# Relational graph convolution on one core: the aggregation buffer with relations outermost, ScalarE writing it with a step, TensorE reading runs of 72

## The reference, cut to what matters

```python
N, F_in = x.shape                    # 6250 nodes, 128 features, float32
R = W_rel.shape[0]                   # 65 relations; 200000 edges, sorted by dst
seg  = dst * R + edge_type
sums = segment_sum(x[src], seg, N * R).reshape(N, R, F_in)
cnt  = segment_sum(ones, seg, N * R).reshape(N, R, 1)
agg  = sums / maximum(cnt, 1.0)      # a mean for each (node, relation)
h = einsum('nri,rio->no', agg, W_rel) + x @ W_root + bias + x @ W_res + b_res
h = relu(batchnorm_over_nodes(h) * gamma + beta)
out = layernorm_over_features(x + h)
```

## Time and profile before

| | value |
|---|---|
| median of three runs | 2689.86 us |
| the profiled execution | 2688.44 us |
| its span (first to last instruction) | 2686.7 us |
| PE busy | 2594.1 us (97%) |
| DVE busy | 1681.9 us (63%) |
| POOL busy | 1471.8 us (55%) |
| ACT busy | 1311.1 us (49%) |
| mean granted TensorE clock | 0.993 of 2.4 GHz |

### The profile page before, as it was taken

How to read it: one execution, slowest core, us unless ns; L and a number is a source line. 1 busy time by engine, 2 the same in 40 slices (tenths; PEclk the granted TensorE clock), 3 DMA queues, 4 the chain that set the end, 5 groups by cost and what they waited for, 6 DMA issues and landing times.

```text
span 2686.7 us, 42326 instructions
## 1 busy us (share of the span) xinstructions
PE 2594.1 (97%) x12868; PEld 2271.2 (85%) x12868; DVE 1681.9 (63%) x5648; ACT 1311.1 (49%) x2427; POOL 1471.8 (55%) x1581
## 2 busy tenths in 40 slices
PE   2899999999999999999999999999999999999995
PEld 1688888888888888888888888888888888888884
DVE  4866666666666666666666665666666666666624
ACT  1545545545554454554545544545454454454523
POOL 2555555555555555555555555555555655555510
PEclk9999999999999999999999999999999999999998
DMA  8645454554445545444444554545545454554421
GB/s 293 175 122 138 117 131 124 131 131 121 130 121 133 132 117 136 119 129 127 127 130 116 138 132 117 136 116 131 138 117 131 121 134 125 123 131 114 116 72 49
DMA packets 262850, 345.30 MB, mean 129 GB/s; under 512 B 29051, under 2 KB 245311, under 8 KB 249439
## 3 DMA queue, kind: packets, MB, share of 16 engines
q0 software_dynamic: 225072, 204.97, 33.8%
q1 hardware_dynamic: 37551, 137.59, 15.3%
HBM read 328.84 MB, written 13.60 MB: 127 GB/s over the span
## 4 chain that ended last, share of the span: by engine, by line
PE 96%; DMA 1%; DVE 1%; ACT 1%; issue 1%; SPq 0%; POOL 0%; ACTq 0%; DVEq 0%; POOLq 0%
PE tb L571 65%; PE ps L546 21%; PE ps L552 8%; DMA xtab<-agg 1%; PE tb L530 1%; ACT agg L729 0%; PE tb L531 0%; DVE bst L1016 0%; PE ps L631 0%; DMA xg<-xtab,srcT 0%; DMA agg<-in_x_dram 0%; PE ps L632 0%; DVE agg L755 0%; PE tb L520 0%; PE prep L509 0%
## 5 line engine op out<-in xcount | busy, mean ns | idle before, releaser
L475 POOL DMA_INDIRECT xg<-xtab,srcT x1563 | 1467.7, 939 | 1096.4 <-PE ps L552 500.5
L571 PE MATMUL tb<-agg,wsb 128*128 128x144 f32 x6370 | 1972.2, 448 | 1.4 <-issue 1.4
L858 DVE TENSOR_SCALAR onehot<-iota,segT,v 128x456 fp32r<-128x456 f32 x1173 | 874.7, 746 | 856.1 <-PE ps L552 695.9
L662 ACT ACTIVATE agg<-ps 128x390 f32 (+1 forms) x1563 | 775.5, 496 | 1246.7 <-PE ps L552 970.8
L571 PEld LDWEIGHTS tb<-agg,wsb 128*128 128x128 f32 x6370 | 1167.8, 201 | 151.2 <-issue 1.5
L546 PE MATMUL ps<-onehot,xg 128*128 128x390 f32 (+1 forms) x3126 | 1155.0, 453 | 37.9 <-DMA xg<-xtab,srcT 35.1
L546 PEld LDWEIGHTS ps<-onehot,xg 128*128 128x128 f32 x3126 | 639.3, 207 | 191.8 <-DMA xg<-xtab,srcT 35.8
L832 DVE TENSOR_SCALAR_CACHE_REDUCE junk<-keyb,keyT 128x256 bf16<-128x256 f32 x1563 | 713.2, 471 | 2.7 <-DMA keyb<-keyd 2.7
L552 PEld LDWEIGHTS ps<-onehot,xg 128*128 128x128 f32 x2930 | 539.9, 189 | 3.8
L552 PE MATMUL ps<-onehot,xg 128*128 128x66 f32 x2930 | 448.0, 234 | 0.0
L651 ACT ACTIVATE onehot<-dist,v,negv 128x456 fp32r<-128x456 f32 x390 | 299.4, 768 | 36.9 <-ACT dist L646 0.7
(11 more groups left out here) (107 smaller groups left out, 353.4 us busy)
## 6 DMA issues: line engine op xcount, KB each, us to landing
keyb<-keyd SPq DMA_DIRECT2D x98, 1088.0 KB
xg<-xtab,srcT POOLq DMA_INDIRECT x1563
xtab<-agg SPq DMA_DIRECT2D x4, 1536.0 KB
hinit<-H SPq DMA_DIRECT2D x1, 3125.0 KB
agg<-in_x_dram SPq DMA_DIRECT2D x4, 768.0 KB, 9.0
out_dram<-agg SPq DMA_DIRECT2D x6, 448.0 KB, 3.0
srcr<-in_src_dram SPq DMA_DIRECT2D x12, 64.0 KB
dstr<-in_dst_dram SPq DMA_DIRECT2D x12, 64.0 KB
```

The costliest lines, as they stand in the source:

```text
L475: pool.indirect_dma_start(out=xg[c % RING][:], out_offset=None, in_=xtab.bitcast(F32R), in_offset=bass.IndirectOffsetOnAxis(ap=srcT[t % 2] ...
L571: ins = nc.tensor.matmul(o, wsb[:, r * F:(r + 1) * F], pair_rhs(p, r), start=(r == 0), stop=(r == R - 1))
L662: nc.scalar.activation(agg_group(g)[:, bass.ds(off, w)], ps[c % 4][:, 0:w], ACT.Copy).then_inc(evac, 1)
L858: nc.vector.tensor_scalar(onehot[o][:].rearrange("p (a b) -> p a b", a=3), iota3[:, :, 0:IW], segT[t % 2][:, k:k + 1], v[:, g % 2, j:j + 1 ...
```

## The change: relations outermost, the two groups' nodes side by side

In a half of `agg`, the column of relation `r`, group `g` (0 or 1) and node `n` is now `r * 156 + g * 78 + n`. The size is the same.

- `pair_rhs` reads, for one relation, 72 adjacent words of group 0, leaves out 6, and reads 72 adjacent words of group 1.
- `evacuate` reads PSUM as before, in order, and writes for each of 6 (or 7) nodes 65 words that are 156 words (624 bytes) apart. The number of elements is the same.
- The offset is now in nodes, so one small DVE instruction that multiplied it by 65 falls away (13 times in all), with the semaphore step before it. Nothing else is added, removed or moved: PE, ACT, POOL and SP issue the same instructions in the same order.

```diff
     OW = (SLOTS + 1) * R + 1
-    GREG = (WIN + SLOTS) * R
-    PREG = 2 * GREG
+    GN = WIN + SLOTS
+    PREG = 2 * GN * R
...
         def agg_group(g):
 
-            base = (g // 2 % 2) * PREG + (g % 2) * GREG
-            return agg[:, base:base + GREG]
+            base, n = (g // 2 % 2) * PREG, (g % 2) * GN
+            return agg[:, base:base + PREG].rearrange("f (r n) -> f n r", r=R)[:, n:n + GN, :]
...
             def turn_offsets(t):
                 pe.wait_ge(offc_rdy, t + 1)
-                nc.tensor.matmul(prep[0:1, 0:P], tc(T_OFF65), ident[:], start=True, stop=True)
+                nc.tensor.matmul(prep[0:1, 0:P], tc(T_OFF2), ident[:], start=True, stop=True)
...
             def pair_rhs(p, r):
                 a = (p % 2) * PREG
-                return agg[:, a:a + PREG].rearrange("f (g n r) -> f g n r", g=2, r=R)[:, :, 0:WIN, r]
+                return agg[:, a:a + PREG].rearrange("f (r g n) -> f r g n", r=R, g=2)[:, r, :, 0:WIN]
...
             def evacuate(c, off):
                 p, g = c // (2 * GC), c // GC
-                w = OW - 1 if last_of_group(c) else W6
+                n = SLOTS + 1 if last_of_group(c) else SLOTS
...
-                nc.scalar.activation(agg_group(g)[:, bass.ds(off, w)], ps[c % 4][:, 0:w], ACT.Copy).then_inc(evac, 1)
+                nc.scalar.activation(agg_group(g)[:, bass.ds(off, n), :],
+                                     ps[c % 4][:, 0:n * R].rearrange("f (n r) -> f n r", r=R), ACT.Copy).then_inc(evac, 1)
...
-                    offs = registers(offrow[t % 2][0:1, k:k + 4], ENG.Activation, (WIN - 1) * R)
+                    offs = registers(offrow[t % 2][0:1, k:k + 4], ENG.Activation, WIN - 1)
...
-                at = step(nc.vector.tensor_scalar(tc(T_OFF2), tc(T_OFF), 0.0, float(WIN - 1), ALU.max, ALU.min))
-                dve.wait_ge(dstep, at)
-                nc.vector.tensor_scalar(tc(T_OFF65), tc(T_OFF2), float(R), None, ALU.mult)
+                nc.vector.tensor_scalar(tc(T_OFF2), tc(T_OFF), 0.0, float(WIN - 1), ALU.max, ALU.min)
```

More of the change, by code:

```diff
@@ L163, in gnn @@
         (B_BIAS, B_RES, GAM, BET, BSUM, BAD, MV, STD, SCL, SHF) = (0, 1, 2, 3, 4, 5, 6, 8, 9, 10)
-        (T_B, T_NEXT, T_B65, T_LAST, T_BG, T_OFF, T_LASTG, T_OFF2, T_OFF65, T_RISE) = range(10)
+        (T_B, T_NEXT, T_B65, T_LAST, T_BG, T_OFF, T_LASTG, T_OFF2, T_RISE) = range(9)
         XST = (XT + 1) * 2 * F
```

## The result

The changed kernel takes 2514.64 us (median of 4 runs, 2509.71 to 2516.89), the kernel before 2689.49 us beside it: a ratio of 0.9347, 95% interval 0.9330 to 0.9363. That is 6.5% faster. The forecast was 2282 us with a range of 2080 to 2430, so the direction was right and the size was not: 233 us of the expected gain of 408 are missing. The profiled run had a span of 2513.6 us.

The account below looks back on a forecast made before the run. PE's pace bounded the kernel; after the change ACT would, at 1.36 us per chunk. Start 118, loop 2081, 6 to the last products, 18 for them, 55.8 to the end: 2279, with 1.7 and 1.4 added 2282 us, range 2080 to 2430.

Parts of the forecast that it names:

- The W_r products: PE's L571 products: reading runs of 72 adjacent words cuts each from 0.2615 to 0.127 us, PE's chunk to 1.07 us.
- ACT's stepped write: ACT's evacuation into SBUF: writing with a step takes 901 ns, 0.408 us more, making ACT's chunk 1.36 us.
- split into 199 ns and 1.80 ns per element: ACT's evacuation: 199 ns fixed plus 1.80 ns for each of 390 stepped elements, 901 ns together.
- SBUF and not the engine sets the price: Stepped access: DVE's writing (1.94 ns) and PE's reading (1.82) cost nearly the same, so 1.80 ns was taken for ACT.
- ACT as the bound: The loop: ACT sets the pace at 1.36 us per chunk (1.26 to 1.60), time 2282 us, chance 66%.
- ACT without idle time in the loop: Sign of being right: ACT's evacuations follow each other by their length plus 0.17 us.
- I am wrong if ACT's cycle grows by something other than the write: Stated sign of failure: ACT's four-chunk cycle lengthening by anything but its evacuations' stepped write.
- the 0.67 us of spare time per chunk: ACT's cover before the change: PE's 1.62 us per chunk less ACT's 0.95.
- Rival 1: POOL's gathers, 1.244 us apart, set the loop's pace if the stepped evacuation stays under 787 ns: 2089 us, chance 18%.
- Rival 3: PE's clock falls to half where PE idles behind ACT: 2770 us if half the time, 2400 one in eight; chance 8%.
- Rivals 2 and 4: ACT's evacuation over 1.17 us makes the kernel slower, 2740 us, 4%; runs of 72 stream no faster, 2690 us, 4%.
- 1.71 ns per column: The skill page's DVE price, tried for ACT's evacuation: 866 ns, 1.32 us per chunk, some 2230 us in all.

Follow-up runs that it names:

- write_only: Changed kernel with the old read, so only ScalarE's stepped write against the kernel before: 2694.22 us, ratio 1.0015.
- pool_on_evac: Changed kernel, but GpSimd waits before every fourth gather on evac, not agg_ps: 2211.59 us, ratio 0.8235 to the kernel before.
- dve_all: Changed kernel, but VectorE makes all one-hots and ScalarE only evacuates: 2088.83 us, ratio 0.7776 to the kernel before.
- filler: Changed kernel plus one float32 product per chunk into an unused PSUM bank, to keep TensorE busier: 2524.84 us, ratio 0.9392 to the kernel before.
- own_semaphore: Changed kernel, but GpSimd waits on its own semaphore, raised by TensorE at each chunk's first product: 2519.55 us, ratio 0.9354 to the kernel before.
- wait_on_memset: Changed kernel, but GpSimd's wait on agg_ps stands at a small memset ahead of every fourth gather: 2623.44 us, ratio 0.9752 to the kernel before.
- wait_each: Changed kernel, but GpSimd waits on agg_ps before every gather instead of once for four: 2475.14 us, ratio 0.9201 to the kernel before.
- read_only: Kernel before with only TensorE's new read of 72-word runs, ScalarE writing adjacent words as before: 2478.14 us, ratio 0.9211.
- read_dve_all: Kernel before with only TensorE's new read, and all one-hots made by VectorE: 2514.63 us, ratio 0.9341.
- no_gather: Changed kernel with only the first 16 gathers, their rows multiplied again for all later chunks: 2210.56 us, ratio 0.8229 to the kernel before.

## Why the prediction was wrong

- **The W_r products: right.** 0.1245 us each against 0.127, from where they run alone; PE's part at full clock is hidden behind ACT, as forecast.
- **ACT's stepped write: right as a sum.** 907 ns against 901; ACT's own cycle is 1.337 us per chunk against 1.36. write_only shows that this write costs next to nothing (0.15%) while PE is slow. Its split into 199 ns and 1.80 ns per element, and the reason that SBUF and not the engine sets the price, no run shows: the two shapes give (990 - 907) / 65 = 1.28 ns per further element in the changed kernel, and the same sum 1.06 in pool_on_evac and 1.86 in dve_all.
- **ACT as the bound: right only where nothing is seen late.** pool_on_evac has a loop step of 1.321 and takes 2211.59 us; the forecast of 2282 is 3% over it. 0.039 us too much per chunk are 60 us of the 71, and the rest lies ahead of the loop and behind it, some 5 us each. With the same prices the forecast would have held the time of this one-word variant.
- **The step that failed: "ACT without idle time in the loop".** The sum took for the loop 1530 times ACT's cycle, so it assumed that an engine whose input is ready goes on at once, and put the way of a finished product to ACT at nothing. Instead ACT and DVE are repeatedly left waiting for chunks that PE has finished up to 8 us earlier, PE then runs out of its four banks, and the two stand still together. 106 late evacuations with 299 us stand against a loop that is 300 us longer than that of pool_on_evac, and against 2514.64 - 2211.59 = 303 us in all. The profile of before had it already, in 56 late evacuations between 200 and 2000 us, of which the view shows six as "remote". They cost nothing, as PE was ahead by its banks, and I passed them over. "I am wrong if ACT's cycle grows by something other than the write" is the sign that came true. The cover that went with the change wasn't the 0.67 us of spare time per chunk that I counted for ACT, but PE's lead.
- **Rival 1 (POOL the bound, 2089):** not what happened, since the write cost more than 787 ns. But its price for POOL's pace was right, as dve_all shows (2088.83; the last microseconds by luck).
- **Rival 3 (the clock):** the clock did fall (0.912), as it said, and in stretches after PE's stalls. It wasn't the cause: filler had more clock and no less time, and pool_on_evac runs at half clock for 123 us of its loop without a loss.
- **Rivals 2 and 4** are out by 907 ns and 16.19 us.
- The Trainium skill's 1.71 ns per column for a hopping destination of VectorE (Vector Engine (DVE) Microarchitecture Reference, section 5.2), used for ACT, gave 866 ns; the trace has 907. It would have made the forecast 2230, which is closer to 2211 and misses the 2514.64 by more.

What stays open is why the increments are seen late. Ruled out are the clock (no loss in pool_on_evac at half clock; filler), the shared semaphore (own_semaphore), the gather as the held instruction (wait_on_memset), one wait for four gathers (wait_each), a high mean load on the DMA engines (pool_on_evac has more of it; bursts weren't tested), ACT's stepped write (read_only), one-hots on ACT (read_dve_all) and a POOL that is held (at none of the 106 late products). It is gone as well in no_gather, which has neither gathers in the loop nor POOL's waits, so that either may be what is needed. Fast W_r products aren't needed for it (56 late in the kernel before, 57 in write_only), only for it to cost time.

## What to carry to other kernels

When a change takes away the slack of the bounding engine, look in the trace of before for waits that end by nothing the profile shows, or by work that was long done, however little they cost there: they are hidden by that engine's lead, and become time when the lead is gone. When the sum of right prices misses the time, move one wait or one piece of work to another engine before changing the arithmetic; here a word (agg_ps to evac) was worth 12%, and the same word cost 8% in a sibling kernel, so it has to be measured in each version. The layout change paid fully only together with a rebalancing: stepped write on ScalarE, all one-hots on VectorE, 2088.83 us.

## What the runs showed of the hardware

- TensorE's float32 products read their moving side at a pace set by the layout in SBUF: a step of 260 bytes between columns 0.2615 us per 144 columns, runs of 72 adjacent words 0.1245 us. That is at 2.4 GHz. At 1.2 GHz the two lie close together: 0.246 and, behind the stall shown above, (292.39 - 291.46) / 4 = 0.23 us.
- ScalarE's write with a step (the same 390 elements from PSUM) takes 907 ns instead of 493, and 455 elements 990 instead of 542. How much of it is fixed and how much goes by element isn't shown.
- With gathers by GpSimd in the loop, other engines can see TensorE's increments up to 8 us after the product ended, several at once (four within 0.28 us in the place shown). In the changed kernel none of the 106 late ones fell due while GpSimd was held in a wait. I had not expected this at all.
- A longer step on an engine that isn't the bound can make the whole faster (dve_all 2088.83 with 920 ns evacuations, read_dve_all 2514.63 with 496).
